# A graph-network kernel: four of every eight target one-hots move from VectorE to ScalarE in pass 1, and the last tile group does its packs before it waits for its gathered rows

## The reference

```python
edge_index = jnp.stack([src, dst])
h = jnp.maximum(_layernorm(x, axis=-1), 0.0)
x = x + _L0_gnn_ref(h, edge_index, edge_weight, ...)   # two layers, both with _aggregate
h = jnp.maximum(_layernorm(x, axis=-1), 0.0)
x = x + _L1_gnn_ref(h, edge_index, edge_attr_64, ...)  # attention, 4 heads
h = jnp.maximum(_layernorm(x, axis=-1), 0.0)
x = x + _L2_gnn_ref(h, ..., src, dst)                  # attention, 8 heads
h = jnp.maximum(_layernorm(x, axis=-1), 0.0)
x = x + _L3_gnn_ref(h, edge_index, ...)                # two layers of gated sums

def _aggregate(h, row, col, edge_weight):
    d = jax.ops.segment_sum(jnp.ones_like(edge_weight), col, num_segments=N)
    val = edge_weight * jax.lax.rsqrt(d[col]) * jax.lax.rsqrt(d[row])
    return jax.ops.segment_sum(val[:, None] * h[row], col, num_segments=N)
```

## Time and profile before

| | us |
|---|---|
| median of 3 runs | 3535.09 |
| lowest and highest | 3529.31, 3539.81 |
| the profiled execution's own time | 3526.88 |
| its span, from first to last instruction | 3525.0 |

### The profile page before, as it was taken

The page is one execution under the profiler, slowest core; times in us unless marked ns, Lnnn a source line. Parts: engine busy times, 40 slices in busy tenths (PEclk is TensorE's granted clock), DMA queues, the critical chain, the costliest instruction groups (busy, mean ns, idle before and its releaser), DMA issues.

```text
span 3525.0 us, 60164 instructions
## 1 busy us (share of the span) xinstructions
PE 2205.9 (63%) x15246; PEld 1969.1 (56%) x15273; DVE 2399.7 (68%) x7660; ACT 1283.6 (36%) x3489; POOL 2004.9 (57%) x2076
## 2 busy tenths in 40 slices
PE   4992240566665567677556676545455455999998
PEld 3991230455554355555445575535455453998998
DVE  7997960777776669999726556575778777433434
ACT  4220020223332123333357767735777774000000
POOL 1777777777776477777267777716777770000000
PEclk9995555676666655555656556667777777999999
DMA  2210000111113123333333333224444441221222
GB/s 82 69 59 4 4 22 27 48 53 52 53 52 48 53 72 93 92 92 92 41 97 82 81 77 80 68 27 149 130 132 131 130 114 24 73 76 52 69 75 63
DMA packets 171637, 250.17 MB, mean 71 GB/s; under 512 B 52006, under 2 KB 120412, under 8 KB 171154
## 3 DMA queue, kind: packets, MB, share of 16 engines
q0 software_dynamic: 72704, 138.94, 16.2%
q1 hardware_dynamic: 94276, 96.20, 9.2%
q10 hardware_dynamic: 4430, 12.43, 1.0%
HBM read 217.00 MB, written 30.41 MB: 70 GB/s over the span
## 4 chain that ended last, share of the span: by engine, by line
POOL 48%; PE 21%; issue 18%; DVE 9%; DMA 2%; ACT 2%; DVEq 1%; POOLq 0%; ACTq 0%; SPq 0%
POOL arena L715 20%; POOL pool L715 17%; PE psum L1504 8%; POOL rec_dram L692 7%; PE psum L1500 5%; POOL ACC L715 3%; PE psum L1230 2%; DVE ACC L2336 1%; PE psum L1268 1%; DVE arena L2062 1%; ACT pool L816 1%; PE psum L1105 1%; DVE pool L2324 1%; DMA arena<-tab_dram,tblk 1%; DVE pool L1725 1%
## 5 line engine op out<-in xcount | busy, mean ns | idle before, releaser
L715 POOL DMA_INDIRECT arena<-tab_dram,tblk x832 | 796.6, 957 | 411.1 <-issue 250.8
L692 POOL DMA_INDIRECT rec_dram<-arena,ACC x400 | 396.1, 990 | 196.5 <-issue 118.9
L715 POOL DMA_INDIRECT pool<-tab_dram,arena x416 | 401.3, 965 | 131.4 <-issue 126.5
L1551 PE MATMUL psum<-pool 128*128 128x136 f32 (+1 forms) x1664 | 361.4, 398 | 82.8 <-DVE pool L2260 76.6
L1551 PEld LDWEIGHTS psum<-pool 128*128 128x128 f32 x1664 | 335.0, 289 | 94.9 <-issue 57.6
L1382 PE MATMUL psum<-pool 128*128 128x128 f32 x832 | 193.0, 426 | 294.6 <-DMA pool<-tab_dram,arena 206.9
L2116 DVE CAST pool<-pool 128x1024 f32<-128x1024 uint8 x264 | 182.4, 694 | 278.1 <-PE psum L1504 168.1
L2062 DVE TENSOR_SCALAR arena<-fwd,arena 128x128 bf16<-128x128 bf16 x2112 | 359.1, 287 | 0.8 <-PE psum L1424 0.8
L1382 PEld LDWEIGHTS psum<-pool 128*128 128x128 f32 x832 | 179.8, 328 | 299.0 <-DVE pool L2129 129.9
L715 POOL DMA_INDIRECT pool<-tab_dram,tblk x272 | 263.9, 970 | 125.5 <-issue 80.2
L857 ACT ACTIVATE arena<-psum,key 128x128 bf16<-128x128 f32 x416 | 146.4, 377 | 473.5 <-PE psum L1325 473.5
(11 more groups left out here) (373 smaller groups left out, 4891.7 us busy)
## 6 DMA issues: line engine op xcount, KB each, us to landing
pool<-items_dram SPq DMA_DIRECT2D x264, 128.0 KB, 2.1
pool<-dst_dram SPq DMA_DIRECT2D x104, 256.0 KB, 3.5
items_dram<-pool SPq DMA_DIRECT2D x132, 128.0 KB, 2.0
arena<-tab_dram,tblk POOLq DMA_INDIRECT x832
HN<-in_edge_attr_dram ACTq DMA_DIRECT2D x23, 500.0 KB
pool<-tab_dram,arena POOLq DMA_INDIRECT x416
rec_dram<-arena,ACC POOLq DMA_INDIRECT x400, 2.1
pool<-tab_dram,tblk POOLq DMA_INDIRECT x272
```

What stands on the lines that cost most here:

```text
L692: nc.gpsimd.indirect_dma_start(rec_dram, bass.IndirectOffsetOnAxis(ap=row_all[:, c:c + 1], axis=0), rec_all[:, c, :], None).then_inc(s_sca ...
L715: nc.gpsimd.indirect_dma_start(to[:, j, :], None, tab_dram[k], bass.IndirectOffsetOnAxis(ap=idx[:, G * g + j:G * g + j + 1], axis=0)).then ...
L1551: last_ = nc.tensor.matmul(bank[j // 3][:, (j % 3) * ww:(j % 3 + 1) * ww], OHF[:, half, j, :], weighed[k][:, half, j, :], start=True, stop ...
```

## The change

A constant `BY_ACT = 4` comes in. VectorE leaves out the last four target one-hots (e = 1, j = 4 to 7) of each pack. ScalarE makes them in a new function `targets`: four Squares of 128x128 with a bias column, a wait for the last of them, and one Relu over all 512 columns. `keep` for pack b first makes the targets of pack b + 1, and then waits for pack b's parts and copies them. TensorE's second part waits for the new semaphore `s_itema`. Part 0 uses the one-hots 0 to 3 and part 1 the one-hots 4 to 7.

In the last group (group 51) TensorE does all six pack parts ahead of the waits for the one-hots and the gathered rows, and then the eight gather products in one go. ScalarE's loop is one turn shorter, and its last three packs are written out.

```diff
+BY_ACT = 4
@@ ScalarE, item_counts
+                def targets(b, slot):
+
+                    lo = P * (PACK - BY_ACT)
+                    for j in range(PACK - BY_ACT, PACK):
+                        last = nc.scalar.activation(onehots[slot][1][:, P * j:P * (j + 1)], iota[:, 0:P], ACT.Square, scale=-1.0,
+                                                    bias=ends[1][:, bass.ds(PACK * b + j, 1)])
+                    last.then_inc(s_itema, 1)
+                    act.wait_ge(s_itema, 2 * b + 1)
+                    nc.scalar.activation(onehots[slot][1][:, lo:PACK * P], onehots[slot][1][:, lo:PACK * P], ACT.Relu, scale=-1.0,
+                                         bias=ones[:, 0:1]).then_inc(s_itema, 1)
+
                 def keep(b, slot, i, peeled):
 
+                    if there(b + 1, PACKS):
+                        targets(b + 1, (slot + 1) % PACKS_A_GROUP)
                     for part in range(2):
                         act.wait_ge(s_itemp, P_PICKS + 2 * b + part + 1)
...
                 act.wait_ge(s_dst, 32)
+                targets(0, 0)
                 for b in range(PACKS_A_GROUP):
                     keep(b, b, 0, True)
-                with act.Fori(1, PACKS // PACKS_A_GROUP, 1) as i:
+                with act.Fori(1, PACKS // PACKS_A_GROUP - 1, 1) as i:
...
-                for b in range(PACKS // PACKS_A_GROUP * PACKS_A_GROUP, PACKS):
+                for b in range(PACKS - PACKS_A_GROUP, PACKS):
@@ TensorE, pack_items
                 if part == 0:
                     pe.wait_ge(s_itemv, V_TILES + 2 * b + 2)
+                else:
+                    pe.wait_ge(s_itema, 2 * (b + 1))
@@ TensorE, long_pass
+                    between = [(b, at, part) for b, at in packs(g, slot, i) if there(b, PACKS) for part in range(2)]
+                    if isinstance(g, int) and g == GROUPS - 1:
+                        for b, at, part in between:
+                            pack_items(b, at, part)
+                        between = []
                     pe.wait_ge(s_ohw, G * (GROUPS + g + 1))
                     pe.wait_ge(s_slot[slot], long_loads(slot, i))
-                    between = [(b, at, part) for b, at in packs(g, slot, i) if there(b, PACKS) for part in range(2)]
@@ VectorE, item_onehots
                 for e in range(2):
-                    for j in range(PACK):
+                    for j in range(PACK - BY_ACT * e):
```

More of the change, by code:

```diff
@@ L465, in gnn_kernel @@
         s_itemc = sem("s_itemc")
+        s_itema = sem("s_itema")
         s_kept_items = [sem(f"s_kept_items{i}") for i in range(PACKS_A_GROUP)]
```

## The result

The changed kernel takes 3579.84 us (median of 4 runs, 3576.7 to 3580.25), the kernel before 3532.41 us (median of 4, 3529.31 to 3539.81). The ratio is 1.0129, with a 95% interval of 1.0112 to 1.0145: slower by 1.3%, or 47 us. The profiled execution took 3576.7 us, with a span of 3574.9.

A forecast was written before the change was run, and what follows sets the result against it. GpSimd's 10.05 us a group, beside VectorE, bounds pass 1; ScalarE's 3.73 us a pack, 11.2 a group, would exceed it. Later copies 41.3 plus last group 1.3 make 42.6 us, added to 3535.1: 3577 us, range 3556 to 3592.

The forecast's parts named there:

- The bound: Pass 1: GpSimd's gathers and VectorE both take about 10.05 us a group, so relieving VectorE alone is worth nothing.
- Steps 1 and 2: ScalarE's targets for a pack: four Squares up to the Relu 1.29 us, then the Relu's step of 0.63 us.
- Steps 3 to 5: ScalarE's copy of part 0, 0.60 us; handover to TensorE and back, 0.70; copy of part 1, 0.51 after overlap.
- 130 cycles: Pass 1's full ScalarE cycles at 3.73 us a pack, making the last copy end 41.3 us later.
- the tail: End of pass 1: six more gather products behind the last part, about +1.3 us.
- the clock's case: Evener load keeps TensorE at full clock, handover 0.49 us, cycle 3.52, about 3550 us; chance 0.10.
- the longer cycle: Part 0 not ready when the Relu ends, or Squares' writes don't overlap: cycle 4.0 us, about 3612 us; chance 0.14.
- The clock: TensorE's granted clock in pass 1 stays at 0.50 nearly throughout, with TensorE about 65% busy.
- The last group: Group 51's rows land long before TensorE reaches it, so its new order saves nothing; GpSimd does not wait for slots.
- The rival without a loss: ScalarE's cycle stays under the gathers' pace, deciding at 3.35 us; pass 1 gains 5.6 us, about 3527 to 3530; chance 0.09.

The follow-up runs named there:

- e1: Changed kernel with the four Squares between the two copies and the Relu behind the second: 3527.88 us against 3529.15 for the kernel before, ratio 0.9999.
- e3: Changed kernel with ScalarE making two of the eight targets, not four: 3526.96 us, ratio 0.9995 to the kernel before.
- e8: Changed kernel without the last group's new order, on the slow chip: 4828.65 us, ratio 1.0183 to the kernel before there (4741.25 us).
- e2: Changed kernel with ScalarE making three of the eight targets, not four: 3527.34 us, ratio 0.9994 to the kernel before.
- e10: Changed kernel with the Squares between the copies, and padding records naming row 24 x lane, not row 0: 3511.15 us, ratio 0.9946 to the kernel before.
- e11: Changed kernel with two targets on ScalarE, and padding records naming row 24 x lane, not row 0: 3513.11 us, ratio 0.995 to the kernel before.
- e9: Kernel before with only the padding records changed, naming row 24 x lane in place of row 0: 3511.65 us against 3531.01, ratio 0.9945.

## Why the prediction was right

Slower by 44.6 on the medians of this result (3577 against 3532.4) was forecast, or 42.6 by the sum; it was 47.4. The measured 3579.8 lies in the forecast's own range of 3556 to 3592. That the time is only 2 to 3 us above the forecast is in part luck: the loss was 5 us more than the sum, and the median of the kernel before, on which the sum was put, came out 2.7 us lower with a fourth run. The mechanism is as forecast, ScalarE's in-order cycle over GpSimd's pace. Point by point:

**The bound.** GpSimd's pace was the bound before, with VectorE beside it. e1 to e3 take 2 to 4 one-hots a pack off VectorE and are within 0.1% of before, so VectorE's relief shows no gain, as said. Its busy row over the pass fell by 359.1 - 274.3 = 84.8 us (the one-hots, L2062 before and L2084 now); I had 90.

**Steps 1 and 2, the targets.** Predicted: a Square's step 0.292 and 1.29 us to the Relu, the Relu 0.72 with a step of 0.63. The summary of the two lines (duration in ns, lowest, median, highest):

```profile
L887 ACT ACTIVATE arena<-iota,arena x528: 384/390/403, 1267.9 to 1766.3; 128x128 bf16<-128x128 f32 x176
L891 ACT ACTIVATE arena<-arena,ones x132: 721/721/722, 1269.2 to 1766.7; 128x512 bf16<-128x512 bf16 x132
```

0.721 us, and in the timeline 1.30 (1641.03 to 1642.33) and 0.62. The estimate from the nearest rows held.

The estimate by the Trainium skill ("ScalarE: Activation LUTs", What ACT_TABLE_LOAD costs) was 0.71 and is 2% under the row; the cycle by it adds up to 3.72, not 3.71 as I had.

**Steps 3 to 5, the copies and the handover.** This is the term that was mis-sized. Predicted: 0.70 us between the end of a copy and the start of the next. Measured: 0.77 in every cycle. From start to start the two copies are 1.35 us apart where I had 1.30. The other terms together are 0.03 to 0.04 us shorter than I had, since the first copy takes 0.58 and not 0.60, the Relu's step is 0.62, and the second copy's 0.49.

My reading of the 0.70 was too narrow to begin with. Of the 132 second copies before, 67 come after 0.70 us, 44 after 0.79 (the pack whose first part has two gather products behind it) and 19 after 0.49. TensorE and ScalarE in the timeline of before, in group 42, and TensorE in that of the changed kernel:

```profile
1620.45 0.61 PE L1424 MATMUL psum<-arena 128*128 128x128 bf16 x4 [0.16 <-ACT pool L887]
...
1622.49 0.60 ACT L887 ACTIVATE pool<-psum 128x512 uint8<-128x512 f32 x1 [0.79 <-PE psum L1424]
```

```profile
1643.67 0.59 PE L1442 MATMUL psum<-arena 128*128 128x128 bf16 x4 [0.92 <-ACT pool L902]
```

In the changed kernel the second part starts 0.14 us after the end of the first part's copy (1643.53 to 1643.67), in all 132 packs. Before, it was 0.05 (1619.10 to 1619.15). The change gives this part a second wait ahead of its matmuls (`s_itema`), long met by then, which fits. But the first part had two waits before already, and it starts 0.05 us after a copy in the groups of TensorE's loop (1620.40 to 1620.45) and 0.14 in those written out. So the second wait is not the whole cause, and the cause of the 0.07 us stays open.

Over the 130 cycles 3.77 against 3.73 is 5.2 us. From the first copy's start to the last one's end it was 494.6 us, where I had 489.4. This is the difference between 42.6 and 47.8, with the tail as predicted: +1.24 us for a predicted 1.3, and e8 shows that it is the new order's.

**Slips in the working.** The 130 full cycles run from the first copy of pack 0, not of pack 1; the sum is right. The range of 3556 to 3592 doesn't take in the clock's case of 3550, as the text beside it says, and the longer cycle is 3612 in one place and 3604 in another.

**The clock.** 0.50 in the whole stretch, as predicted, in the earlier trace rows 0.57. TensorE was busy for 329.9 of 500 us (66%; I had 65%). The case of the clock going up is out.

**The last group.** TensorE reached its parts at 1761.90, 55 us after the last gather was issued. The order could not help there. GpSimd did not wait for its slots, as predicted, but not by much: the slot of group 51 was free for 15 us, where that of group 15 had been free for 66.

**The rival without a loss.** Its turning point at a cycle of 3.35 us held well: 3.37 costs nothing, 3.77 costs 47 us. But its gain of 5.6 us was wrong where the cycle is short enough. It said that TensorE would start the last group's parts ahead of the last landing and that only eight products would follow. It left out that those parts stand behind group 50's landing, and that a copy waits for a store, which beside the padding's gathers took 8.25 us. e1 ends its pass 1.3 us earlier than before, not 5.6: its last copy ends 2.7 us earlier after the first gather (541.7 against 544.4), and the new order gives half of that back in the tail (3.39 us against 2.00). VectorE was saturated (315.9 of 320 us), and none of the kernels with its work on ScalarE and a cycle under 3.4 us gained clear of noise: e1, e2 and e3 against before, e10 and e11 against e9.

The Trainium skill ("Perfetto Trace Analysis", Optimizing Scalar/DVE Operations) says that offloading may make sense if DVE is saturated; these runs show a case in which that condition was met and nothing was gained.

**What stays open.** What lengthens the handover from 0.70 to 0.77 us, what stops the engines on the slow chip, and how much each of the later passes gets of the 5.7 us.

## What to carry to other kernels

An engine's idle time is not its free capacity: add up the in-order cycle, with the handovers that the new work can't fill, and hold that against the pace of the engine that bounds. Here the same instructions cost 47 us ahead of the copies and nothing between them. If two engines share the bound, relief for one alone gains nothing. And look at what padding fetches: lookups that all name row 0 were the slowest transfers of the kernel, and 128 different rows gave 18 to 20 us for two added VectorE instructions.

## What the runs showed of the hardware

- A 2 KB packet of an indirect gather that reads one DRAM row again and again took 0.74 us of a DMA engine, one that reads different rows 0.12. Stores on another queue are slow beside them too: one of 128 KB landed after 8.25 us in e1, and from 1694 to 1715 us their median was 5.5 us in before and 1.7 in e9.
- The handover ScalarE, TensorE (four matmuls of 128x128 at a granted clock of 0.50), ScalarE left ScalarE idle for 0.70 us or, behind two gather products, 0.79 in the kernel before, and for 0.77 in every pack of the changed kernel. The added wait ahead of the matmuls, long met, fits this in part.
- A bf16 Relu over 512 columns with a bias column took 721 ns in all 132 cases, and a Square of 128 columns 390, with four in 1.26 us.
- One chip ran every kernel a third slower, with ScalarE stopped mostly for 4 to 6 us once in a group, and instruction times as on the others. GpSimd's gathers then waited for slots that TensorE had yet to free.
